# A graph layer's edge count with the projection h = xn W laid between its matmuls

## The reference

```
xn = layernorm(x)
h  = xn @ W                                    # 1024 x 1024
al, ar = h @ a_l, h @ a_r
e  = exp(-leaky_relu(al[src] + ar[dst], 0.1))
gnn = elu(segment_sum(e * h[dst], src) / (segment_sum(e, src) + 1e-5))
mix = linear attention over 16 heads: qkv = xn @ w_qkv.T, features elu + 1, then w_out, b_out
x  = x + gnn + mix
x  = x + moe(layernorm(x))                     # 8 experts, top 2, and a shared MLP
```

## Time and profile before

| | before |
|---|---|
| median of 3 runs | 3138.7 us (3137.01 to 3142.95) |
| span of the profiled execution | 3134.6 us |
| PE busy | 2988.9 us (95%) |
| DVE busy | 1958.8 us (62%) |
| ACT busy | 1276.0 us (41%) |
| POOL busy | 120.1 us (4%) |
| edge count, first to last matmul | 9.3 to 182.2 us |
| h, from its first matmul to the start of g = 4 | 191.6 to 251.5 us |

### The profile page before, as it was taken

How to read it: one execution, slowest core, us unless ns; L and a number is a source line. 1 busy time by engine, 2 the same in 40 slices (tenths; PEclk the granted TensorE clock), 3 DMA queues, 4 the chain that set the end, 5 groups by cost and what they waited for, 6 DMA issues and landing times.

```text
span 3134.6 us, 45176 instructions
## 1 busy us (share of the span) xinstructions
PE 2988.9 (95%) x16932; PEld 2523.4 (81%) x16932; DVE 1958.8 (62%) x2582; ACT 1276.0 (41%) x1605; POOL 120.1 (4%) x92
## 2 busy tenths in 40 slices
PE   5899999769999999999999999999999999999997
PEld 5789699758887888788878887888788878888876
DVE  6946424556666666666666666666666666666665
ACT  4742122334444444444434444444444444444451
POOL 2230000000000000000000000000000000000001
PEclk8999999889999999999999999999999999999999
DMA  3011010256565665665565556665666566666565
GB/s 102 0 61 55 27 55 28 86 168 224 202 215 198 207 210 202 205 209 201 202 212 202 201 202 212 205 214 202 207 217 215 203 208 210 215 212 207 202 234 165
DMA packets 272154, 548.59 MB, mean 175 GB/s; under 512 B 22944, under 2 KB 88730, under 8 KB 271813
## 3 DMA queue, kind: packets, MB, share of 16 engines
q1 hardware_dynamic: 253762, 532.16, 49.9%
q0 software_dynamic: 18176, 13.50, 1.7%
HBM read 536.88 MB, written 8.70 MB: 174 GB/s over the span
## 4 chain that ended last, share of the span: by engine, by line
PE 84%; DMA 7%; DVE 4%; ACT 2%; issue 2%; SPq 0%; DVEq 0%; ACTq 0%; POOL 0%; POOLq 0%
PE ps L1509 23%; PE ps L1511 23%; PE ps L1510 23%; DMA raw<-in_L_ffn_sd 3%; PE ps L1268 2%; PE ps L1325 2%; PE ps L1326 2%; PE ps L1324 2%; DMA raw<-in_L_ffn_rd 2%; PE ps L1384 1%; DVE c_lo L1127 1%; ACT c_hi L659 1%; DMA wl<-in_L_gnn_W 1%; PE ps L1309 1%; DMA xg<-y_rows,tok_cur 1%
## 5 line engine op out<-in xcount | busy, mean ns | idle before, releaser
L1127 DVE TENSOR_TENSOR c_lo<-raw,c_hi 128x1024 fp32r<-128x1024 f32 x960 | 1125.6, 1220 | 360.9 <-ACT c_hi L659 360.4
L659 ACT CAST c_hi<-raw 128x1024 fp32r<-128x1024 f32 x960 | 953.0, 1047 | 490.6 <-DMA raw<-in_L_ffn_ru 170.0
L1509 PE MATMUL ps<-yT_hi,c_hi 128*128 128x314 f32 (+1 forms) x2048 | 629.6, 307 | 0.0
L1510 PE MATMUL ps<-yT_lo,c_hi 128*128 128x314 f32 (+1 forms) x2048 | 629.5, 307 | 0.0
L1511 PE MATMUL ps<-yT_hi,c_lo 128*128 128x314 f32 (+1 forms) x2048 | 629.0, 307 | 0.0
L1509 PE MATMUL ps<-c_hi,xgT_hi 128*97 128x512 f32 x1024 | 402.8, 393 | 3.6 <-DVE c_lo L1127 3.4
L1511 PE MATMUL ps<-c_hi,xgT_lo 128*97 128x512 f32 x1024 | 403.4, 394 | 0.0
L1510 PE MATMUL ps<-c_lo,xgT_hi 128*97 128x512 f32 x1024 | 401.3, 392 | 0.0
L1509 PEld LDWEIGHTS ps<-yT_hi,c_hi 128*128 128x128 f32 x2048 | 387.3, 189 | 2.8 <-DVE c_lo L1127 0.7
L1510 PEld LDWEIGHTS ps<-yT_lo,c_hi 128*128 128x128 f32 x2048 | 387.5, 189 | 1.3
L1511 PEld LDWEIGHTS ps<-yT_hi,c_lo 128*128 128x128 f32 x2048 | 387.2, 189 | 0.0
(11 more groups left out here) (228 smaller groups left out, 3516.4 us busy)
## 6 DMA issues: line engine op xcount, KB each, us to landing
raw<-in_L_ffn_rg SPq DMA_DIRECT2D x128, 1024.0 KB, 5.4
raw<-in_L_ffn_ru SPq DMA_DIRECT2D x128, 1024.0 KB, 7.0
raw<-in_L_ffn_rd SPq DMA_DIRECT2D x128, 1024.0 KB, 5.5
raw<-in_L_ffn_sg SPq DMA_DIRECT2D x32, 1024.0 KB, 5.6
raw<-in_L_ffn_su SPq DMA_DIRECT2D x32, 1024.0 KB, 5.6
raw<-in_L_ffn_sd SPq DMA_DIRECT2D x32, 1024.0 KB, 6.4
wl<-in_L_mix_w_qkv SPq DMA_DIRECT2D x6, 2048.0 KB, 7.8
wl<-in_L_gnn_W SPq DMA_DIRECT2D x2, 2048.0 KB, 28.4
```

What stands on the lines that cost most here:

```text
L659: nc.scalar.copy(order.view(c_hi[u % RING], u), part(raw[r % RAW])).then_inc(sem("hi_done"), 1)
L1127: V.tensor_tensor(order.view(c_lo[u % RING], u), part(raw[r % RAW]), order.view(c_hi[u % RING], u).bitcast(F32), ALU.subtract).then_inc(se ...
L1509: MM(out_, l_hi, r_hi, start=first, stop=False)
L1510: MM(out_, l_hi, r_lo, start=False, stop=False)
```

## The change

- The loops over the groups of the count are unrolled in TensorE, VectorE and ScalarE. A table `H_WORK` says after which chunk TensorE does a part of the other work: the transposes of xn behind chunks 2 to 18 of group 1, the 20 projections of h from group 1, chunk 9 to group 4, chunk 27, the four turns of g = 4 in groups 4 and 5, the router in group 5. VectorE and ScalarE have their parts at fixed chunks.
- h goes to one PSUM bank (7), so each tile waits until the one before has been copied out. The transposes of xn have two banks rather than three.
- The LayerNorm statistics of all tiles are taken in group 0, the square root once, and the normalizing in group 1.
- v_int and v_lo lie where a_bc lies, so a_bc is loaded behind the last add to C, ahead of b_bc on POOL's queue. The w_parts of g = 5 stand ahead of the al reduction. The albc matmuls move to the end of g = 5 and behind t = 2 of g = 6, the copies to k_map(0, 2) and k_map(0, 4).
- The one-hots are 628 and 316 wide.

```diff
+H_BANK = 7
+H_WORK = {
+    (1, 2): (("turn", 0),), (1, 6): (("turn", 1),), (1, 9): (("first", 0, 0),), (1, 10): (("turn", 2),),
+    (1, 12): (("second", 0, 0),), (1, 14): (("turn", 3),), (1, 15): (("first", 0, 1),), (1, 18): (("second", 0, 1), ("turn", 4)),
+    (1, 21): (("first", 0, 2),), (1, 24): (("second", 0, 2),), (1, 27): (("first", 0, 3),),
+    (2, 4): (("second", 0, 3),), (2, 8): (("first", 0, 4),), (2, 12): (("second", 0, 4),),
+    (2, 24): (("first", 1, 0),), (2, 27): (("second", 1, 0),),
+    (3, 5): (("first", 1, 1),), (3, 10): (("second", 1, 1),), (3, 15): (("first", 1, 2),), (3, 20): (("second", 1, 2),),
+    (3, 27): (("first", 1, 3),),
+    (4, 5): (("second", 1, 3),), (4, 11): (("first", 1, 4),), (4, 16): (("key", 0),), (4, 21): (("key", 1),),
+    (4, 27): (("second", 1, 4),),
+    (5, 4): (("key", 2),), (5, 9): (("key", 3),), (5, 15): (("router",),)}
...
-    wl = [place(f"wl{i}", [P, 4 * D], F32, at=shared_at + i * 16384) for i in range(2)]
+    v_int = place("v_int", [TP, NT, SC], I32, at=a_at)
+    v_lo = place("v_lo", [TP, NT, SC], I32, at=a_at + 6272)
+    wl_at = a_at + 2 * 6272
+    wl = [place(f"wl{i}", [P, 4 * D], F32, at=wl_at + i * 16384) for i in range(2)]
...
-        return TB if n < 2 * NT or n >= YT0 else TB[:2]
+        return TB if n >= YT0 else TB[:2]
...
-        pool.dma_start(a_bc[:], a[0, :].partition_broadcast(TP)).then_inc(sem("a_in"), 16)
         pool.dma_start(rw_in[:], router_w).then_inc(sem("rw_in"), 16)
...
+        pool.wait_ge(sem("counted"), 2 * NG + 2)
+        pool.dma_start(a_bc[:], a[0, :].partition_broadcast(TP)).then_inc(sem("a_in"), 16)
         pool.wait_ge(sem("rwT_ps"), 1)
         pool.dma_start(b_bc[:], b_out.partition_broadcast(TP)).then_inc(sem("b_in"), 16)
...
...
+        count_group(0, {18: lambda: w_hi(0), 27: std})
+        count_group(1, {3: lambda: w_hi(1), 5: lambda: tokens(0), 9: lambda: tokens(1), 14: lambda: tokens(2),
+                        16: lambda: h_out(0, 0), 18: lambda: tokens(3), 21: lambda: (h_out(0, 1), tokens(4)),
+                        27: lambda: h_out(0, 2)})
+        count_group(2, {7: lambda: h_out(0, 3), 16: lambda: h_out(0, 4), 18: lambda: w_hi(2), 21: lambda: w_hi(3)})
+        count_group(3, {3: lambda: h_out(1, 0), 14: lambda: h_out(1, 1), 23: lambda: h_out(1, 2)})
+        count_group(4, {9: lambda: h_out(1, 3), 21: lambda: w_part(G_K, 0), 25: lambda: w_part(G_K, 1)})
+        count_group(5, {3: lambda: h_out(1, 4), 7: lambda: w_part(G_K, 2), 12: lambda: w_part(G_K, 3), 18: router_hi})
...
...
+        count_group(0, {12: lambda: stats(0), 15: lambda: stats(1), 18: lambda: stats(2), 21: lambda: stats(3),
+                        24: lambda: stats(4)})
+        count_group(1, {0: lambda: apply(0), 3: lambda: (apply(1), w_lo(0)), 6: lambda: tokens(0), 7: lambda: apply(2),
+                        8: lambda: w_lo(1), 9: lambda: digits(0), 11: lambda: (tokens(1), apply(3)), 15: lambda: (tokens(2), apply(4)),
+                        19: lambda: tokens(3), 23: lambda: tokens(4)})
+        count_group(2, {9: lambda: digits(1), 19: lambda: w_lo(2), 22: lambda: w_lo(3)})
+        count_group(3, {9: lambda: digits(2)})
+        count_group(4, {9: lambda: digits(3), 22: lambda: w_part(G_K, 0), 26: lambda: w_part(G_K, 1)})
+        count_group(5, {8: lambda: w_part(G_K, 2), 9: lambda: digits(4), 13: lambda: w_part(G_K, 3), 19: router_lo})
...
         digits(NG - 1)
         for i in range(4):
-            w_part(G_K, i)
+            w_part(G_K + 1, i)
         dve.wait_ge(sem("a_in"), 16)
...
-            if t < 4:
-                w_part(G_K + 1, t)
...
-            k_map(0, t, G_K + 2, {0: lambda: albc_copy(0), 1: lambda: albc_copy(1)}.get(t))
+            k_map(0, t, G_K + 2, {2: lambda: albc_copy(0), 4: lambda: albc_copy(1)}.get(t))
...
+        def h_project(half, t, second):
+            g = 2 * half + second
+            group_ready(g)
+            if second == 0 and half * NT + t:
+                pe.wait_ge(sem("h_out"), half * NT + t)
+            if half == 0:
+                pe.wait_ge(sem("turned_lo"), 2 * t + 2)
+            m = project(g, t, xnT_hi, xnT_lo, H_BANK)
+            if second:
+                m.then_inc(sem("h_ps"), 1)
...
-                if g == G_K + 1 and t == 0:
+                if g == G_K + 1 and t == NT - 1:
                     pe.wait_ge(sem("diag_done"), NT)
...
-                if g == G_K + 1 and t == 1:
+                if g == G_K + 2 and t == 2:
                     pe.wait_ge(sem("albc_out"), 1)
```

More of the change, by code:

```diff
@@ L559, in feature_exp, with tokens, h_out, router_hi @@
                                  ACT.Exp).then_inc(sem("fe_done"), 1)
-        act.wait_ge(sem("indices"), 1)
[L562 to L580, removed]
+        def tokens(t):
+            for j in (2 * t, 2 * t + 1):
+                split_hi(j, tokens_part(xnT_hi, xnT_lo, j, j))
+        def h_out(half, t):
+            act.wait_ge(sem("h_ps"), half * NT + t + 1)
+            nc.scalar.copy(h[:, t, half * HALF:(half + 1) * HALF], PS[H_BANK][0:TP, :]).then_inc(sem("h_out"), 1)
+        def router_hi():
+            act.wait_ge(sem("rwT_ps"), 1)
+            act.wait_ge(sem("const_done"), 1)
+            nc.scalar.copy(rw_half(0), PS[H_BANK][:, 0:KT * E].rearrange("p (k n) -> p k n", k=KT)).then_inc(sem("rwT_hi"), 1)
+        act.wait_ge(sem("indices"), 1)
+        count_group(0, {18: lambda: w_hi(0), 27: std})
[6 more added lines that the diff above has]
+        count_group(5, {3: lambda: h_out(1, 4), 7: lambda: w_part(G_K, 2), 12: lambda: w_part(G_K, 3), 18: router_hi})
         for i in range(4):
@@ L789, in w_lo, with count_group @@
                             ALU.subtract).then_inc(sem("w_lo"), 1)
-        def count_group(gr, first, between):
+        def count_group(gr, between):
             for c in range(EG):
@@ L806, in count_group @@
                 if c in between:
                     between[c]()
[L809 to L836, removed]
+        def stats(t):
+            if t == 0:
+                dve.wait_ge(sem("x_in"), 16 * NT)
+            for half in range(2):
+                V.bn_stats(st6[:, t, half, :], resid[:, t, half * HALF:(half + 1) * HALF]).then_inc(sem("x_stats"), 1)
+            dve.wait_ge(sem("x_stats"), 2 * t + 2)
+            link(V.bn_aggr(mv[:, t, :], st6[:, t, :, :]))
+            V.tensor_scalar(mv[:, t, 1:2], mv[:, t, 1:2], EPS, None, ALU.add).then_inc(sem("x_var"), 1)
@@ L1339, in _ @@
-        m.then_inc(sem("rwT_ps"), 1)
-        pe.wait_ge(sem("count_out"), NG * NT)
-        for g in range(G_K):
-            group_ready(g)
-            for t in range(NT):
-                if g == 0:
-                    pe.wait_ge(sem("turned_lo"), 2 * t + 2)
-                if g == 2:
-                    pe.wait_ge(sem("h_out"), t + 1)
-                project(g, t, xnT_hi, xnT_lo, t)
-                if g == G_K - 1 and t < 4:
-                    turn(G_K, t)
+            if g >= G_K:
+                m.then_inc(sem("proj"), 1)
@@ new lines, in project, with h_work @@
+            return m
+        def h_project(half, t, second):
+            g = 2 * half + second
+            group_ready(g)
+            if second == 0 and half * NT + t:
[5 more added lines that the diff above has]
+                m.then_inc(sem("h_ps"), 1)
+        def h_work(gr, c):
+            for what, *at in H_WORK.get((gr, c), ()):
+                if what == "turn":
+                    pe.wait_ge(sem("const_done"), 1)
+                    pe.wait_ge(sem("xn_done"), at[0] + 1)
+                    for j in (2 * at[0], 2 * at[0] + 1):
+                        turn_tokens(j, xn[:, at[0], :], j)
+                elif what == "key":
+                    turn(G_K, at[0])
+                elif what == "router":
+                    pe.wait_ge(sem("rw_in"), 16)
+                    pe.wait_ge(sem("h_out"), 2 * NT)
+                    for k in range(KT):
+                        m = TR(PS[H_BANK][:, k * E:(k + 1) * E], rw_in[:, k * P:(k + 1) * P], ident[0:E, 0:E])
+                    m.then_inc(sem("rwT_ps"), 1)
+                else:
+                    h_project(at[0], at[1], int(what == "second"))
@@ L1353, in _ @@
+        for gr in range(NG):
+            count_group(gr)
         for g in range(G_K, G_V):
```

91 lines of the change are left out of this document (40 added, 51 removed).

## The result

The changed kernel takes 3154.0 us (median of 4 runs, 3151.35 to 3159.16) against 3140.6 us before (4 runs): a ratio of 1.005, with a 95% interval of 1.0035 to 1.0064. That is slower by 13.4 us; 10.3 had been forecast. Its profiled execution has a span of 3157.1 us and took 3159.16, the longest of its four, so the shifts are read at fixed places of the program, not at its end.

A forecast was written before the change was run, and what follows sets the result against it. TensorE, holding 84% of the chain of waits, was taken to bound the kernel. An earlier count (-22 us), stalls (+29.6) and low clock (+2.7) summed to +10.3, giving a median of 3149.0 us, range 3124 to 3160.

The forecast's parts named there:

- The end of the count: Edge count with h woven in: group 0 ends near 46.5 us, the first k group can start at 229.5.
- in the same wait: Group 0: the five LayerNorm statistics lie in the wait for W, which was put at 37 us.
- a_bc: Loaded behind the last add on POOL: load taken as 7 us, so al can start at T + 17.5.
- T: Moment the first k group (g = 4) can start: 229.5 us, 22 us earlier than 251.5.
- The collision: During al: GpSimd's five bias adds and VectorE's reduction exclude each other, adding all 11.95 us.
- D: End of al: T + 43.4, or T + 31.5 without collision. As rival: interleaved stretch goes badly, 3159.5 us, chance 0.10.
- The stalls: TensorE in the k stretch waits for VectorE's late splits: 20.7, 4.5, 3.3 and 1.1 us, together 29.6.
- The clock: Behind the first k-stretch stall TensorE runs at half clock for 5.5 us, losing 2.7; nothing added after second and third.
- Sum at the aggregation: Earlier count -22, stalls +29.6, clock +2.7: +10.3 us.
- I carry a shift at 316.4 unchanged to the end: Everything after 316.4 us hangs on TensorE's progress, so the shift there reaches the end unchanged.
- B: Rival for al: bias adds don't hold the reduction, first stall 8.8 us, time 3135, no difference; chance 0.23.
- C: Rival for the count: TensorE's filler covers nearly all waits of the six groups, 3126 us at no idle; chance 0.27.

The follow-up runs named there:

- e5: The changed kernel with the LayerNorm statistics of all five tiles moved behind chunk 27 of group 0: 3155.3 us, ratio 1.0055 to the kernel before.
- e10: e6 with ScalarE's cast of W behind chunk 27 of group 0 instead of chunk 18: 3122.9 us, ratio 0.9949 to the kernel before.
- e11: e6 with both the LayerNorm statistics and the cast of W behind chunk 27 of group 0: 3117.6 us, ratio 0.9928 to the kernel before.
- e1: The changed kernel with GpSimd's five bias adds held until all diag tiles are made: 3142.8 us, ratio 1.0019 to the kernel before.
- e6: The changed kernel with a_bc in its own place, loaded behind group 0's additions, bias adds behind al, al woven between weight splits: 3126.4 us, ratio 0.9966.
- e8: e6 with the LayerNorm statistics behind chunk 27 of group 0: 3124.1 us, ratio 0.9963 to the kernel before.
- e3: The changed kernel with a_bc in its own place, loaded before the count's first group, and bias adds behind the diag tiles: 3144.4 us, ratio 1.0020.

## Why the prediction was right, and what it missed

The direction, the mechanism and nearly all places came out as forecast; each term:

- **The end of the count.** Forecast 229.5, measured 228.25, so -23.2 us instead of -22. Groups 2 to 5 (a projection behind a group's last chunk counted to that group) were forecast at 36.2, 33, 29.8 and 27.5 us and took 36.3, 32.9, 30.3 and 28.8. The first additions to C, forecast at 61.8, came at 58.7. Within group 0 the reading was wrong in its reason. I took W for the one thing that held it and put it at 37. It landed at 34.5, and x at 29.4 held it too, through the statistics that I had laid "in the same wait". e5, e10 and e11 show two waits of nearly equal length; I had looked at one.
- **a_bc.** al could start at T + 17.5 by the forecast; it started at 246.03, T + 17.8.
- **The collision.** D was forecast at T + 43.4 and came at 270.1, T + 41.9: 10.4 us of holding instead of 11.95: each of the five adds held one operation, and each for less than its own length. e1 took it away and got the 14 us of the earlier trace rows. The trace agrees with what the prediction took from the Trainium skill (SBUF — State Buffer, SBUF: two separate sides): the reductions, which read two SBUF tensors, took 3.2 to 3.5 us beside an add, 1.22 without. The diag tiles (one SBUF tensor and a scalar, fp32, 125 wide) were held as well, 2.2 to 2.3 us instead of 0.28, as are the one-hots; so two tensor inputs aren't needed for it here. The same sentence of the Trainium skill names a second kind, a VectorE operation in a 2-port perf mode, which the prediction left out; in which mode the diag tiles and the one-hots ran, no run here shows.
- **The stalls.** 19.1, 4.5 and 3.0, and no fourth, against 20.7, 4.5, 3.3 and 1.1 of the forecast: 26.6 instead of 29.6.
- **The clock** is the term that was mis-sized. I took 2.7 us for the first stall, and nothing for the ones behind it. The k stretch is longer by 6.1 us than its stalls explain. The windows show why: 0.71 behind the first stall, 0.83 at 280 to 290 and 0.67 at 300 to 310, behind a stall of 3, so some 2 us for the first and 4 for the later two. The reason for putting these at nothing, a mean of 1.00 in the count before, was read from one group (78 to 104 us). The later groups of the same trace have the same longest wait, 2.99 us, and windows of 0.93 and 0.84. The changed kernel's count shows it as well: in group 5, behind waits of 3.62 and 2.48 us, TensorE runs at half clock from 211 to 217. In the woven e6, with 1.8 us of stalls, it is 1.00 up to 300, and the rest is 1 us.
- **Sum at the aggregation:** -23.2 + 26.6 + 6.1 = +9.5, against +10.3. That it is so close is in part luck: the count ended 1.2 us earlier and the stalls were 3.0 us shorter than forecast, and 3.4 us more of low clock nearly made up for it.
- **"I carry a shift at 316.4 unchanged to the end"** is the step that failed, by 4 us. From the aggregation to the first gather of an expert the changed kernel takes 320.8 us instead of 316.65. In its profile 1.3 us of it lie between the last feature exponential and the first square root of the LayerNorm (72.0 instead of 70.7): behind the wait for `outT_lo` described at e6, here 1.91 us long, the clock is 0.50 from 532.2 to 535.2, where the kernel before has 1.00. 3.1 lie in the loads of the first expert weights, and 0.3 come back behind them. SyncE's timeline, before and after:

```profile
578.47 10.12 SPq L378 DMA_DIRECT2D y_rows<-y  x5
588.98 1.20 SPq L393 DMA_DIRECT2D raw<-in_L_ffn_sg  x1
590.36 8.15 SPq L393 DMA_DIRECT2D raw<-in_L_ffn_su  x1
```

```profile
589.37 11.13 SPq L392 DMA_DIRECT2D y_rows<-y  x5
600.88 1.73 SPq L407 DMA_DIRECT2D raw<-in_L_ffn_sg  x1
602.79 9.77 SPq L407 DMA_DIRECT2D raw<-in_L_ffn_su  x1
```

The same three issues take 3.2 us longer. All profiles have one of two values for this piece, 18.8 to 19.2 us or 21.8 to 22.1, never one between; why, the runs don't say.

**The rivals.** B (no collision) fell in the profile. e1 is what B described: its first stall is 9.0 us (8.8 forecast for B), but its time 3142.8 is above B's 3135, for the clock as above and the 4 us behind the aggregation. C's mechanism, idle time covered by TensorE's filler, holds only in part: 40.5 us of waits were left in the count, 21.3 in group 0 and 19.2 in the groups behind it, where I had counted 23 and C wanted nearly none. D did not happen.

## What to carry to other kernels

When work is moved out of the way of a busy engine, list what it used to cover: h hid the load of a_bc, the bias adds and the lead of al, and all three came into the open at once, each worth 8 to 14 us at the aggregation in the order in which I took them away. An engine off the critical path (GpSimd, 4% busy) can cost its neighbour one long operation per operation of its own; put such work where the neighbour does PSUM work (0.68 us an operation beside the adds in e1, as without them) or nothing. And where an engine waits at one place, ask what the next engine in line waits for at the same moment: of two waits of nearly equal length, removing either alone gave nothing here (e5, e8, e10), removing both 5 us (e11). And TensorE's clock is a term of its own: several short waits cost more of it here than the one long one.

## What the runs showed of the hardware that was not expected

- A VectorE operation whose tensors all lie in SBUF and that meets a GpSimd addition is held for up to about one whole addition, whatever its own length: 0.28 became 2.2 to 2.3 us, 1.22 became 3.2 to 3.5. Operations with an input in PSUM were not held (0.68 us beside the adds in e1).
- The length of a wait alone doesn't tell what the clock does behind it. Stalls of 3 to 4.5 us went with 0.67 to 0.83 in their windows; waits of 2.99 us in the count before left 1.00 in one group and 0.93 or 0.84 in windows of later ones; and behind a wait of 1.92 us, with the same work ahead, it stayed at 1.00 before and fell to 0.50 for some 3 us in the change and in e6. What decides it the runs don't say.
- A 1000 KB load that spreads one row over 125 partitions, issued at 8.4 us (e3), pushed the landing of x from 29.4 to 34.6.
- The issues of identical loads on SyncE's queue took 3 us more in five kernels than in the other nine: from the last square root to the first cast of an expert's weight 21.8 to 22.1 us in place of 18.8 to 19.2.
